# A split comparison and small maxima on VectorE beside a stream of indirect DMAs

## The chip, the cores and the metric

The kernel runs on one core of a Trainium2 chip. The metric is device time in microseconds (us), from one launch. A NeuronCore has TensorE (PE: matmuls, with its weight loads shown as PEld), VectorE (DVE), ScalarE (ACT), GpSimd (POOL) and SyncE (SP), which run their own instruction streams and meet at semaphores. Transfers are issued from SP, ACT and POOL; the indirect ones (gather and scatter by a list of indices) are issued from POOL.

## The reference

A graph has 6250 nodes with 48 features and 206,250 edges, sorted by destination. Two layers follow each other, each with a residual and a layer norm:

```
deg   = segment_sum(1, src) ;  dinv = rsqrt(deg)
x1    = layernorm(x + segment_sum(x[src] * dinv[src] * dinv[dst], dst))
gate  = silu(edge_attr @ W1.T + b1) @ W2.T + b2
gate += sum(emb[type[src]] * (emb[type[dst]] @ adaptW.T))
cw    = where(distance < 6, 0.5 * (cos(pi * distance / 6) + 1), 0)
msg   = gate * x1[dst] * (cw * node_vec[dst])
agg   = segment_sum(msg, src) / clip(segment_sum(node_vec[dst], src), 1e-8)
out   = layernorm(x1 + (layernorm(x1 + agg) * gamma + beta))
```

A segment sum is done as a matmul with a one-hot matrix: a comparison of indices with the numbers 0 to 127 yields ones where an edge belongs to a node, and TensorE multiplies by it.

## The kernel before, in words

Edges are cut into 101 tiles of 16 columns of 128 edges (NT = 101, G = 16). Three blocks follow each other.

The first (to about 290 us) counts degrees and prepares the tables in DRAM. The third (from about 2815 us) reads the scattered rows and adds them up per node. The change lies in the second, the loop over the tiles, from about 290 to 2815 us. There `over_tiles` (line 83) writes for each engine one list of steps; a step with lag k works in turn t on tile t - k. Six turns are unrolled in a hardware loop (U = 6). The order of the list is the order of the instructions on that engine.

In a turn each engine does this:

- POOL, `gather` (line 714): 16 indirect DMAs (line 722), one per column, each fetching 128 rows of the table by `gidx`; then `scatter` (line 726), one indirect DMA (line 730) that writes the routed rows of the tile 6 before. `gather` waits for `summed` and `gate_used` of the tile 6 before and for its indices.
- PE: the edge network (lines 747 and 759), `pick` (line 777), `routes` (line 821), `ranks`, and last `total` (line 856), which waits for the gathers of this turn and for the one-hot `oh_d`.
- ACT: copies out of PSUM and the splitting into bf16 parts (lines 882 to 970).
- DVE, in this order: `spots` (L1062, a minimum), `keys` (L1165), `product(0)` (L1195 to L1208), `normalize` in every second turn (L1109 to L1139), `steps_of_groups` (L1069), `onehots` (L1047, 2048 numbers a lane into `oh_d`), `buckets` (L1052, 816 numbers into `oh_b`), `route_onehots(0)` (L1089, eight comparisons of 896), `put_rows` (L1078), `add_early` (L1187) and `early_onehots` (L1176, 2048 and 640 numbers into `eoh`), `less_first` (L1148), `less_high(0)` (L1216), `product(1)`, `less_second` (L1156), `places` (L1057, 2048 numbers into `oh_t`), `less_high(1)` (L1216), `less_middle(0)` (L1224), `route_onehots(1)` (eight more of L1089), `less_middle(1)` (L1224).

`add_early` and `early_onehots` work only in the last 51 or so turns (EARLY_FROM = 46): they sum rows of a node group that are already complete.

Of the kernel before, what the change touches and what calls it, by code (L numbers as in the profile page):

```python
# [5 lines left out]
F32 = mybir.dt.float32  # L6
# [3 lines left out]
ALU = mybir.AluOpType  # L10
ACT = mybir.ActivationFunctionType
AX = mybir.AxisListType

P = 128
# [9 lines left out]
G = 16  # L24
# [8 lines left out]
U = 6  # L33
# [13 lines left out]
ECOLS = EARLY * R // P  # L47
# [18 lines left out]
def bc_mid(ap, n):  # L66

    return ap.unsqueeze(1).broadcast_to([ap.shape[0], n, ap.shape[1]])
# [7 lines left out]
def wait_apart(e, sem, value, passed):  # L76


    e.wait_ge(sem, value)
    e.sem_inc(passed, 1)  # L80
# [36 lines left out]
def since(i, s, n):  # L117

    return not isinstance(i, int) or U * i + s >= n
# [6 lines left out]
def build(nc, x, src, dst, edge_attr, edge_weight, node_type, node_vec, W1T, b1, W2T, b2,  # L126
# [14 lines left out]
    with ctx:  # L141
        def sb(name, shape, dt=F32, to=ctx):
            return to.enter_context(nc.sbuf_tensor(name, shape, dt))

        def ps(name, shape, dt=F32, to=ctx):
            return to.enter_context(nc.psum_tensor(name, shape, dt))

        def sem(name, to=ctx):
            return to.enter_context(nc.semaphore(name))

        passed = sem("passed")
        iota_f = sb("iota_f", [P, P])
# [8 lines left out]
        number = sb("number", [P, P, G], BF16)  # L161
        key16 = sb("key16", [P, K], BF16)
        bkt16 = sb("bkt16", [P, K], BF16)
        w16 = sb("w16", [P, K], BF16)
# [28 lines left out]
        with ExitStack() as ph:  # L193
# [67 lines left out]
            with nc.Block() as block:  # L261
                @block.sync
                def _(e):
                    e.dma_start(src_i[:, :], src).then_inc(src_in, 16)
                    e.dma_start(dst_i[:, :], dst).then_inc(dst_in, 16)
                    e.dma_start(nv[:, :], node_vec).then_inc(wl, 16)
                    e.dma_start(xin[:, :, :], x).then_inc(x_in, 16)
                    e.dma_start(b1c[0:C, :], b1).then_inc(wl, 16)
                    e.dma_start(b1c[C:2 * C, :], b1).then_inc(wl, 16)
                    e.dma_start(gam[:, :], gamma.broadcast_to([P, C])).then_inc(wl, 16)  # L270
                    e.dma_start(bet[:, :], beta.broadcast_to([P, C])).then_inc(wl, 16)
                    e.wait_ge(wz, 2)
                    for k in range(2):
                        e.dma_start(w1[RA * k:RA * (k + 1), C * k:C * (k + 1)], W1T).then_inc(wl, 16)
                        e.dma_start(w2[C * k:C * (k + 1), C * k:C * (k + 1)], W2T).then_inc(wl, 16)
                        e.dma_start(w2[2 * C:2 * C + 1, C * k:C * (k + 1)], b2).then_inc(wl, 16)
                    e.wait_ge(mapped, 1)
                    e.dma_start(src_pid, pid_i[:, :]).then_inc(stored, 16)
                    e.wait_ge(dst_done, 1)
                    e.dma_start(dst_pid, dst_i[:, :]).then_inc(stored, 16)  # L280
                    e.wait_ge(blank, 1)
                    e.dma_start(table0[NODE_ROWS:NODE_ROWS + P, :], zeros[:, 0:2 * EX].bitcast(F32)).then_inc(filled, 16)
                    for first in cleared:
                        e.dma_start(slots[R * first:R * (first + CAP - CLEAR), :].rearrange("(p a) c -> p (a c)", p=P),
                                    zeros[:, :]).then_inc(filled, 16)
                    e.wait_ge(types_got, 16 * NP2)
                    e.dma_start(queries.rearrange("p (h c) -> p h c", c=EM), tab[:, :, 0:EM]).then_inc(stored, 16)
                    for k, (a, b) in enumerate(PARTS):
                        e.wait_ge(lows, k + 1)
                        e.dma_start(table0[P * a:P * b, :].rearrange("(h l) c -> l h c", l=P),  # L290
                                    tab[:, a:b, EM:EM + EX]).then_inc(stored, 16)
                    e.wait_ge(wl, 16 * 11)
                    e.wait_ge(filled, 16 * (len(cleared) + 1))
                    e.wait_ge(stored, 16 * (len(PARTS) + 3))
# [268 lines left out]
        with ExitStack() as ph:  # L563
# [5 lines left out]
            oh_d = sb("oh_d", [P, 2, P, G], BF16, ph)  # L569
# [21 lines left out]
            eoh = sb("eoh", [P, P, ECOLS], BF16, ph)  # L591
            ethree = sb("ethree", [P, 3 * MW], F32, ph)
            epart = sb("epart", [P, MW], F32, ph)
            phid = ps("phid", [2 * C, 512], F32, ph)
            gate = ps("gate", [P, 512], F32, ph)
            pwin = ps("pwin", [P, 2, 512], F32, ph)
# [22 lines left out]
            erows_in, ecopied, emade, esummed, eout = (  # L619
                sem(n, ph) for n in ("erows_in", "ecopied", "emade", "esummed", "eout"))  # L620
# [18 lines left out]
            def visit(i, s):  # L639

                return U * i + s - EARLY_FROM
# [6 lines left out]
            def visits(i, s):  # L648

                return 0 <= visit(i, s) < NB if isinstance(i, int) else True  # L650

            def pair_of(i, s):

                return i * (U // 2) + s // 2

            with nc.Block() as block:
# [383 lines left out]

                @block.vector
                def _(e):
                    def onehots(i, s):
                        t = U * i + s
                        if since(i, s, 2):
                            e.wait_ge(summed, t - 1)
                        e.tensor_tensor(oh_d[:, s % 2], number[:, :, :], bc_mid(w16[:, bass.ds(t * G, G)], P),  # L1047
                                        ALU.is_equal).then_inc(ohd, 1)

                    def buckets(i, s):  # L1050
                        t = U * i + s
                        e.tensor_tensor(oh_b[:, :, :], number[:, 0:NB, :], bc_mid(bkt16[:, bass.ds(t * G, G)], NB),  # L1052
                                        ALU.is_equal).then_inc(ohb, 1)

                    def places(i, s):
                        e.wait_ge(row_in[s % 2], 16 * (pair_of(i, s) + 1))
                        e.tensor_scalar(oh_t[:, s % 2], oh_t[:, s % 2], iota_p[:, 0:1], None, ALU.is_equal  # L1057
                                        ).then_inc(oht, 1)

                    def spots(i, s):  # L1060
                        e.wait_ge(ranked, U * i + s + 1)
                        e.tensor_reduce(spot[:, s % 2, :], ranks_of.rearrange("p b q -> p q b"),  # L1062
                                        AX.X, ALU.min).then_inc(placed, 1)
# [103 lines left out]
                    def early_onehots(i, s):  # L1167
                        if not visits(i, s):
                            return
                        v = visit(i, s)  # L1170
                        wait_apart(e, ecopied, 2 * v + 1, passed)
                        if not isinstance(v, int) or v > 0:
                            e.wait_ge(esummed, v)
                        for a in range(0, ECOLS, G):
                            b = min(a + G, ECOLS)
                            oh = e.tensor_tensor(eoh[:, :, a:b], number[:, :, 0:b - a], bc_mid(emine[:, a:b], P),  # L1176
                                                 ALU.is_equal)
                        oh.then_inc(emade, 1)

                    def add_early(i, s):  # L1180
                        if not visits(i, s):
# [38 lines left out]
                    def less_middle(m):  # L1220
                        def step(i, s):
                            n = 2 * (U * i + s) + m
                            e.wait_ge(mid, n + 1)
                            e.tensor_tensor(parts[:, s % 2, m * HC:(m + 1) * HC, 2 * MW:2 * MW + C], val[:, m],  # L1224
                                            parts[:, s % 2, m * HC:(m + 1) * HC, MW:MW + C],
                                            ALU.subtract).then_inc(split_ok, 1)
                        return step

                    steps = [0]
# [31 lines left out]
                    with when(e, 1):  # L1261
                        over_tiles(e, NT, U, (spots, 5), (keys, 5), (product(0), 5), (normalize, 2), (steps_of_groups, 5),
                                   (onehots, 0), (buckets, 4), (route_onehots(0), 5), (put_rows, 5),
                                   (add_early, 7, EARLY_FROM), (early_onehots, 6, EARLY_FROM), (less_first, 2),
                                   (less_high(0), 5), (product(1), 5), (less_second, 2), (places, 4),
                                   (less_high(1), 5), (less_middle(0), 5), (route_onehots(1), 5),
                                   (less_middle(1), 5))
# [479 lines left out]
```

## Time and profile before

| | us |
|---|---|
| median of 3 runs | 3051.34 (3043.43 to 3051.47) |
| the profiled execution | 3027.21 |
| its span, first to last instruction | 3025.4 |
| POOL busy in the span | 2121.9 (70%) |
| DVE busy | 2404.3 (79%) |
| PE busy | 2250.1 (74%) |
| ACT busy | 1395.5 (46%) |

The span is what the profiler saw between the first and the last instruction. Engine, line and tile names are those of the program; the line is where the instruction was written. In a row of the timeline the first number is the start in us from the span's start, the second how long it took; what stands in brackets is the idle time of the engine before it and what ended it, and "issue" there means that it waited for nothing that the profile shows. Neighbouring instructions on DVE can overlap by up to 0.1 us, as the next starts while the last drains.

### The profile page before, as it was taken

What the parts mean: (1) busy time and instruction counts of PE and PEld (TensorE: products, weight loads), DVE (VectorE), ACT (ScalarE), POOL (GpSimd) and SP (SyncE); (2) the same over time, 40 slices, a digit from 0 to 9 for tenths busy, and PEclk for the clock granted to TensorE, in tenths of its full rate; (3) what the DMA queues carried; (4) which work ended last, traced back from release to release, by engine and by line L of the source; (5) the groups of instructions that cost most, each with busy time, mean ns of one, the idle gap of its engine ahead of it and who ended that gap; (6) DMA issues with size and microseconds to landing.
All of it is one profiled execution on the core that took longest, in us unless ns stands there. A gap on an engine that the chain in (4) does not pass through costs nothing. (4 is left out here: it accounts for less than half of the span.)

```text
span 3025.4 us, 73628 instructions
## 1 busy us (share of the span) xinstructions
PE 2250.1 (74%) x25909; PEld 1913.9 (63%) x25909; DVE 2404.3 (79%) x5424; ACT 1395.5 (46%) x2929; POOL 2121.9 (70%) x1852
## 2 busy tenths in 40 slices
PE   6980476678777787777787877787878787788475
PEld 5760365566666666655666666676767666667475
DVE  9994577777787777877788897888888878887698
ACT  7982244444444444444444444444444444445123
POOL 7506777877777777777777777777777777760165
PEclk9765688888888888988888898888989888979797
DMA  8405233333433434333344454444444444442896
GB/s 322 148 2 163 62 112 108 101 126 116 127 113 115 127 115 124 117 112 112 118 148 153 143 155 146 147 145 145 145 147 147 144 144 145 156 138 103 333 389 224
DMA packets 174987, 441.53 MB, mean 146 GB/s; under 512 B 92662, under 2 KB 92662, under 8 KB 154806
## 3 DMA queue, kind: packets, MB, share of 16 engines
q1 hardware_dynamic: 103754, 236.05, 23.4%
q0 software_dynamic: 67888, 194.98, 20.7%
q10 hardware_dynamic: 3004, 5.90, 0.6%
q8 instruction: 219, 3.59, 0.5%
q14 instruction: 122, 1.00, 0.1%
HBM read 292.51 MB, written 144.27 MB: 144 GB/s over the span
## 5 line engine op out<-in xcount | busy, mean ns | idle before, releaser
L722 POOL DMA_INDIRECT slot<-table,gidx x1616 | 1811.9, 1121 | 633.6 <-issue 620.2
L821 PEld LDWEIGHTS route<-parts,oh_r 128*128 128x128 bf16 x11312 | 764.9, 100 | 91.6 <-issue 66.9
L821 PE MATMUL route<-parts,oh_r 128*128 128x148 bf16 x11312 | 812.9, 232 | 3.2 <-DVE parts L1224 3.0
L1089 DVE TENSOR_SCALAR oh_r<-iota_r,spot 128x896 bf16<-128x896 f16 x1616 | 613.5, 451 | 74.4 <-PE route L821 74.4
L894 ACT ACTIVATE routed<-route 128x444 bf16<-128x444 f32 (+1 forms) x1010 | 507.9, 513 | 258.5 <-PE route L821 240.0
L856 PE MATMUL pwin<-slot,oh_d 128*128 128x144 bf16 x1616 | 167.6, 276 | 404.2 <-DMA slot<-table,gidx 372.1
L856 PEld LDWEIGHTS pwin<-slot,oh_d 128*128 128x128 bf16 x1616 | 147.8, 155 | 428.2 <-issue 270.0
L777 PEld LDWEIGHTS pwin<-win,oh_t 128*128 128x128 bf16 x4848 | 262.3, 117 | 200.6 <-issue 101.8
L777 PE MATMUL pwin<-win,oh_t 128*128 128x80 bf16 (+1 forms) x4848 | 277.0, 227 | 77.1 <-ACT ssum L904 71.6
L747 PE MATMUL phid<-attr,w 80*96 80x512 f32 x404 | 282.2, 789 | 44.4 <-issue 44.1
L1195 DVE TENSOR_TENSOR prod<-slot,got 128x256 f32<-128x256 f32 x202 | 84.6, 419 | 231.3 <-ACT parts L955 231.2
L759 PE MATMUL gate<-w,hid 97*128 97x96 f32 x1616 | 251.0, 305 | 1.6 <-ACT hid L882 1.6
L949 ACT ACTIVATE got<-pwin 128x640 f32<-128x640 f32 x202 | 142.0, 703 | 230.3 <-PE pwin L777 227.0
L759 PEld LDWEIGHTS gate<-w,hid 97*128 97x128 f32 x1616 | 225.9, 216 | 3.4 <-ACT hid L882 2.8
L730 POOL DMA_INDIRECT slots<-routed,sidx x101 | 116.5, 1153 | 115.1 <-ACT routed L894 76.9
L962 ACT ACTIVATE parts<-val 128x384 bf16<-128x384 f32 x202 | 104.5, 517 | 198.2 <-DVE val L1208 198.2
L882 ACT ACTIVATE hid<-phid,b1c 96x512 f32<-96x512 f32 x202 | 137.5, 681 | 119.9 <-PE phid L747 117.1
L1692 PE MATMUL acc<-rows,onehot 128*128 128x147 bf16 x1785 | 136.4, 239 | 68.1 <-issue 37.8
L323 ACT ACTIVATE by_col<-oh_hi 128x832 bf16<-128x832 bf16 x101 | 178.7, 1794 | 16.3 <-DVE oh_lo L463 12.5
L1176 DVE TENSOR_TENSOR eoh<-number,emine 128x2048 bf16<-128x2048 bf16 x102 | 102.8, 1057 | 99.8 <-ACT emine L981 99.6
L1692 PEld LDWEIGHTS acc<-rows,onehot 128*128 128x128 bf16 x1785 | 130.9, 143 | 73.6 <-issue 73.6
L356 PEld LDWEIGHTS deg<-by_col,oh_lo 128*128 128x128 bf16 x1616 | 108.9, 165 | 53.8 <-ACT by_col L323 53.2
(228 smaller groups left out, 3257.3 us busy)
## 6 DMA issues: line engine op xcount, KB each, us to landing
rows<-slots SPq DMA_DIRECT2D x51, 1295.0 KB, 8.8
oh_t<-dst_row SPq DMA_DIRECT2D x101, 512.0 KB
erows<-slots SPq DMA_DIRECT2D x51, 777.0 KB
attr<-in_edge_attr SPq DMA_DIRECT2D x101, 320.0 KB
slots<-zeros SPq DMA_DIRECT2D x53, 518.0 KB
slot<-table,gidx POOLq DMA_INDIRECT x1616
table<-tab SPq DMA_DIRECT2D x3, 676.0 KB, 5.9
weight_t<-weights SPq DMA_DIRECT2D x101, 8.0 KB
```

Of the source, the lines that this page charges most:

```text
L323: e.activation(by_col[:, s % OR], oh_hi[:, s % OR].rearrange("p b g -> p g b"), ACT.Copy).then_inc(laid, 1)
L722: e.indirect_dma_start(out=slot[:, s, g, :], out_offset=None, in_=table0, in_offset=bass.IndirectOffsetOnAxis(ap=gidx[:, s, g:g + 1], axis ...
L747: e.matmul(phid[:, :], w1[:, :], attr[:, s % 2, 512 * m:512 * (m + 1)], start=True, stop=True).then_inc(hidden, 1)
L759: mm = e.matmul(gate[:, 2 * C * k:2 * C * (k + 1)], hid[:, P * c:P * (c + 1)], w2[:, :], start=True, stop=True)
L777: mm = e.matmul(pwin[:, g // 4, first:first + n], oh_t[:, s % 2, m * HC + g, :], win[:, s, AT[k]:AT[k] + n], start=(k == 0), stop=(k == 2) ...
L821: mm = e.matmul(route[:, (NPH * m + phase) % 2, RC * (j - a):RC * (j - a + 1)], oh_r[:, c, slot_of, :], parts[:, s % 2, c, :], start=(c == ...
L856: mm = e.matmul(sums, oh_d[:, s % 2, :, g], rows[:, g, :], start=(g == 0), stop=(g == G - 1))
L882: e.activation(hid[0:2 * C, 512 * m:512 * (m + 1)], phid[:, :], ACT.Silu, bias=b1c[:, 0:1]).then_inc(hid_sb, 1)
L894: e.activation(routed[:, s % 2, RC * (HS * m + a):RC * (HS * m + b)], route[:, (NPH * m + phase) % 2, 0:RC * (b - a)], ACT.Copy).then_inc( ...
L949: e.activation(got[:, m].rearrange("p (b k) c -> p b k c", b=2), by_bank[:, :, :, 0:WX], ACT.Copy)
L1089: oh = e.tensor_scalar(oh_r[:, c], iota_r[:, :, :], spot[:, s % 2, c:c + 1], None, ALU.is_equal)
L1692: mm = e.matmul(acc[:, b % 2, 0:3 * MW], onehot[:, b % OS, :, c], rows[:, b % RS, c, 0:3 * MW], start=(c == 0), stop=(c == COLS - 1))
```

## The change

VectorE's comparison for `oh_d` is done in two halves, each of 64 of the 128 numbers (1024 elements a lane instead of 2048); the semaphore `ohd` is raised by the second. A helper `let_in` issues a maximum of two numbers per lane (a `tensor_reduce` of 128x2 to 128x1 in f32, without a wait and without a semaphore) into a small tensor of its own, `aside`. It stands behind each half of `oh_d`, behind `oh_b`, `oh_t`, both comparisons of `eoh`, and behind `less_middle(0)`. Nothing reads `aside`. That makes five such instructions in each of the 101 turns and two more in each of 51.

```
+            aside = sb("aside", [P, U, 8], F32, ph)
...
+                    def let_in(s, n):
+                        e.tensor_reduce(aside[:, s, n:n + 1], iota_f[:, 0:2], AX.X, ALU.max)
...
                     def onehots(i, s):
...
-                        e.tensor_tensor(oh_d[:, s % 2], number[:, :, :], bc_mid(w16[:, bass.ds(t * G, G)], P),
-                                        ALU.is_equal).then_inc(ohd, 1)
+                        for a in range(0, P, P // 2):
+                            oh = e.tensor_tensor(oh_d[:, s % 2, a:a + P // 2], number[:, a:a + P // 2, :],
+                                                 bc_mid(w16[:, bass.ds(t * G, G)], P // 2), ALU.is_equal)
+                            if a:
+                                oh.then_inc(ohd, 1)
+                            let_in(s, a // (P // 2))
                     def buckets(i, s):
...
+                        let_in(s, 2)
                     def places(i, s):
...
+                        let_in(s, 3)
...
(early_onehots)
-                        oh.then_inc(emade, 1)
+                            if b == ECOLS:
+                                oh.then_inc(emade, 1)
+                            let_in(s, 4 + a // G)
...
(less_middle)
+                            if m == 0:
+                                let_in(s, 7)
```

## Rows read from the trace of the kernel before

**Rows 1.** The page's head, and groups of POOL by line, 320 to 2600 us.
```profile
span 3025.4 us, 73628 instructions
...
L722 POOL DMA_INDIRECT slot<-table,gidx x1497 | 1673.3, 1118 | 476.5 <-issue 463.1 <-DMA gidx<-src_pid 9.7 <-DVE val L1201 3.7
L730 POOL DMA_INDIRECT slots<-routed,sidx x90 | 103.1, 1146 | 27.4 <-issue 26.8 <-DMA gidx<-src_pid 0.6
```

**Rows 2.** Two stretches of the loop: length, then each engine's busy us (instructions), clock, DMA.
```profile
320.00:1400.00 1080.00, 806.50 (x9136) 673.62 (x9137) 818.58 (x2075) 482.88 (x1077) 847.90 (x762) 0.86 0.38 114
1400.00:2600.00 1200.00, 955.91 (x11025) 811.27 (x11023) 992.89 (x2415) 551.48 (x1280) 928.41 (x825) 0.88 0.47 144
```

**Rows 3.** Timeline of POOL: two free gathers, two stretched, the last one.
```profile
1499.15 0.94 POOL L722 DMA_INDIRECT slot<-table,gidx  x1 [0.30 <-issue]
1500.40 0.94 POOL L722 DMA_INDIRECT slot<-table,gidx  x1 [0.30 <-issue]
...
1507.92 1.59 POOL L722 DMA_INDIRECT slot<-table,gidx  x1 [0.30 <-issue]
1509.81 1.11 POOL L722 DMA_INDIRECT slot<-table,gidx  x1 [0.30 <-issue]
...
2702.43 0.94 POOL L722 DMA_INDIRECT slot<-table,gidx  x1 [0.30 <-issue]
```

**Rows 4.** Timeline of DVE beside the gather of 1507.92.
```profile
1507.47 1.21 DVE L1047 TENSOR_TENSOR oh_d<-number,w 128x2048 bf16<-128x2048 bf16 x1
1508.61 0.57 DVE L1052 TENSOR_TENSOR oh_b<-number,bkt 128x816 bf16<-128x816 bf16 x1
```

**Rows 5.** Timeline of POOL: gathers held back longest, and the last beside oh_d.
```profile
346.14 5.17 POOL L722 DMA_INDIRECT slot<-table,gidx  x1 [0.30 <-issue]
...
950.94 2.27 POOL L722 DMA_INDIRECT slot<-table,gidx  x1 [0.30 <-issue]
...
1456.23 5.69 POOL L722 DMA_INDIRECT slot<-table,gidx  x1 [0.30 <-issue]
...
1711.52 2.52 POOL L722 DMA_INDIRECT slot<-table,gidx  x1 [0.30 <-issue]
...
2597.40 1.07 POOL L722 DMA_INDIRECT slot<-table,gidx  x1 [0.30 <-issue]
```

**Rows 6.** Timeline of DVE beside the gathers of 950.94, 1456.23 and 1711.52.
```profile
951.81 0.57 DVE L1052 TENSOR_TENSOR oh_b<-number,bkt 128x816 bf16<-128x816 bf16 x1
...
1457.07 2.98 DVE L1089 TENSOR_SCALAR oh_r<-iota_r,spot 128x896 bf16<-128x896 f16 x8
1459.98 0.20 DVE L1078 TENSOR_SCALAR sidx<-rank,iota_p 128x1 int32<-128x1 f32 x1
...
1461.13 0.42 DVE L1198 TENSOR_REDUCE logit<-prod 128x8 f32<-128x256 f32 x1
...
1711.36 2.00 DVE L1176 TENSOR_TENSOR eoh<-number,emine 128x2048 bf16<-128x2048 bf16 x2
```

**Rows 7.** Groups of DVE with their shapes: the comparison to be split, its neighbour, less_middle.
```profile
L1047 DVE TENSOR_TENSOR oh_d<-number,w 128x2048 bf16<-128x2048 bf16 x101 | 122.1, 1210 | 15.2 <-PE pwin L856 15.0
...
L1224 DVE TENSOR_TENSOR parts<-val,parts 128x384 bf16<-128x384 f32 x202 | 111.0, 550 | 0.0
...
L1052 DVE TENSOR_TENSOR oh_b<-number,bkt 128x816 bf16<-128x816 bf16 x101 | 57.4, 568 | 0.0
```

**Rows 8.** Timeline of DVE: a very small instruction and the one behind it.
```profile
1522.56 1.00 DVE L1062 TENSOR_REDUCE spot<-rank 128x16 f32<-128x816 f32 x1
1523.47 0.19 DVE L1165 COPY parts<-key 128x16 bf16 x1
1523.55 0.42 DVE L1195 TENSOR_TENSOR prod<-slot,got 128x256 f32<-128x256 f32 x1
```

**Rows 9.** Waits of PE from 700 to 1500 us: us in total, times, longest.
```profile
PE pwin L856 <- DMA slot<-table,gidx: 138.6, 31, 8.8
```

**Rows 10.** Waits of PE, then of DVE, from 1500 to 2400 us.
```profile
PE pwin L856 <- DMA slot<-table,gidx: 84.0, 34, 5.3
...
DVE eoh L1176 <- ACT emine L981: 61.9, 22, 5.9
```

## The prediction

> **What bounds the kernel now.** I first asked which engine never waits inside the loop. The groups of POOL from 320 to 2600 us show it [rows 1]: 1497 gathers and 90 scatters are busy for 1673.3 + 103.1 = 1776 us, and of the idle 476.5 + 27.4 = 504 us nearly all is "issue". The timeline tells what that idle time is: 0.30 us ahead of each gather [rows 3], and 1587 x 0.30 = 476 us. So POOL takes one indirect DMA after another and waits for hardly anything else: it sets the pace, although VectorE and TensorE are as busy in the same stretches [rows 2]. The waits of TensorE say the same from the other side: `total` waits for the gathered rows 31 times in 800 us and 34 times in 900 us, nearly once a turn, for 138.6 and 84.0 us [rows 9, 10].
>
> A free gather takes 0.94 us and the next starts 1.25 us later [rows 3]. A turn of 17 such would be 21.2 us. It is longer, since many gathers are stretched: 1673.3 - 1497 x 0.94 = 266 us in the 2280 us [rows 1], to which the scatters add some 14. That 280 us is all that the change can win on POOL; with 94 turns in the stretch it is 3.0 us a turn.
>
> What stretches them is read by laying the two timelines side by side. The gather of 1507.92 ends at 1509.51, 0.83 us behind the end of `oh_d` (1508.68) [rows 3, 4]. The gather of 1456.23 ends at 1461.92, 0.79 us behind the start of the first `TENSOR_REDUCE` that follows [rows 5, 6]. So a gather does about 0.15 to 0.2 us, then needs something that a long VectorE comparison holds, and needs some 0.75 us after it got it. In both of these cases VectorE ran on at its usual pace meanwhile (`oh_b` 0.57 against its mean of 0.568 [rows 4, 7]): the way is needed for an instant, and VectorE loses nothing by giving it.
>
> The end of an instruction does not always open the way. The gather of 1507.92 got in between `oh_d` and `oh_b`; that of 950.94 did not, and ended 0.83 us behind the end of `oh_b` (952.38) [rows 5, 6]; that of 1456.23 was passed over at the end of `oh_d`, `oh_b`, all eight `oh_r` and the four instructions behind them. Such starved gathers of over 5 us number 8, the first at 346.14 and the last at 1456.23 [rows 5].
>
> Going through the timeline from 320 to 2600 us with this point (0.19 us behind a gather's start), I put the 280 us down to the VectorE instruction that ran there. `oh_d`: 93 gathers, the first at 346.14 and the last at 2597.40 [rows 5], 90 us, of which the 8 starved make 37. The `oh_r` trains: 350 gathers, 71 us, such as the 0.17 us of 1509.81 [rows 3]. `eoh`: 44 gathers, 33 us, such as the 1.58 us of 1711.52 [rows 5, 6]. `less_middle`: 86 gathers, 26 us. `oh_t`: 75 gathers, 18 us. The rest, f32 products and subtractions, 42 us.
>
> **The change part by part.** If a gather's need falls anywhere in a held stretch of L us with equal chance, it waits L/2 on average and the chance is L/1.25, so a turn pays L x L / 2.5.
>
> *`oh_d` in halves, with maxima.* The slope between 816 and 2048 elements is (1210 - 568) / 1232 = 0.52 ns an element [rows 7], so a half of 1024 is 0.68 us, and 0.60 us from start to start, since neighbours overlap (`oh_d` 1.21 long, next start after 1.14 [rows 4]). Now: one stretch of 1.2 us and one of 0.57. If the boundary always opened this would be (1.44 + 0.3) / 2.5 = 0.7 us a turn; never opened, the first need falls on average 0.62 us into the 1.77, and the gather waits 1.14 us. Measured is 90 / 94 = 0.96. Then: three stretches of 0.6, 0.6 and 0.5: (0.36 + 0.36 + 0.25) / 2.5 = 0.39 us a turn. Gain 0.57 us x 94 = 54 us. Bounds: if no maximum ever opens more than a plain boundary does, the starved 37 us stay and the rest falls from 53 to 37 us, a gain of 16; at most all 90 go.
>
> *The maximum in `eoh`.* The comparisons of 1.2 and 0.7 us become separate stretches: (1.44 + 0.49) / 2.5 = 0.77 us against 33 / 47 turns = 0.70 now. By the formula nothing is won; only the cases like 1711.52, which missed the middle opening, about a dozen of the 44, gain 0.6 us each. I take 6 us; bounds 0 and 15.
>
> *Behind `less_middle(0)`.* It ends a run of f32 work before the second `oh_r` train. One 0.47 us stretch costs 0.09 a turn, 8 us for 94 turns, and there are two; 26 us are paid now. I take 7 us; bounds 0 and 20.
>
> *Behind `oh_t`.* The opening there works already as far as I see (75 gathers, 0.25 us each; the formula for 0.75 us gives 0.22 a turn, 21 us). I take 0; bounds -3 and 8.
>
> *What stays.* The 71 us in the `oh_r` trains and the 42 us of the f32 work are untouched.
>
> *What VectorE pays.* A maximum of two numbers: the nearest rows are a reduce of 816 at 1.00 us and a copy of 16 at 0.19, behind which the next starts after 0.08 us [rows 8]. I take 0.08 us; bounds 0.08 and 0.19. Five a turn, and the split adds 0.06: 0.46 us a turn, 0.62 with the two of `eoh`. Over 101 and 51 turns that is 46 + 8 = 54 us of VectorE's time (up to 120). What hides it is the wait for POOL. In 700 to 1500 us `total` waits 138.6 us in some 33 turns, 4.2 us a turn; in 1500 to 2400, 84.0 in 37, 2.3 a turn [rows 9, 10]. POOL's turn shrinks by 0.7, VectorE's loop grows by 0.6: 1.3 of the 2.3 are used. So the second half is near the edge but not over it. Queued behind each maximum is only the next VectorE step; TensorE's `total` gets `ohd` about 0.15 us later, which lies inside its wait for the gathers. The cover ends with the last gather at 2703.37 [rows 3]: the drain of six turns pays 6 x 0.5 = 3 us.
>
> Sum: 54 + 6 + 7 = 67 us, less 3 for the drain, gives 64. From this I take off 12: in turns with the early sums VectorE already waits 61.9 us for ScalarE's `emine` in 900 us [rows 10], a loop that POOL does not set, and in some of these turns the end will not be POOL's. So -52 us, and the profiled execution of 3027.21 becomes 2975. The profiled execution lay 24 us below the median of the runs; I carry the difference over to the median: 3051.34 - 52 = 2999 us.
>
> **A rule against it.** The rows show a gather passed over at more than ten boundaries [rows 5, 6]. The Trainium skill, "SBUF — State Buffer", section "SBUF: two separate sides", says that the port pair shared by VectorE and GpSimd is an exclusive lock held for a whole instruction, and that the blocked side goes on at VectorE's end plus about 115 ns. By that rule a maximum between two comparisons opens nothing that the end of the comparison did not open. The 5.17 to 5.69 us of the starved gathers disagree; the 0.83 us behind `oh_d` and `oh_b` agree with its other half. Its result is the second rival below.
>
> **The rivals.**
>
> *More than forecast.* Gathers and VectorE's steps run in step with each other (the 0.30 us gap and the fixed order), so one removed stretch can free others: a gather that isn't late at `oh_d` may miss the `oh_r` train's first members too. If a third more goes, 67 becomes 95, less 3: 3051 - 92 = 2959. For: the starved gathers come in the same place each time. Against: the `oh_r` trains cost 0.2 us a gather whatever comes before.
>
> *The maxima open nothing.* A window of 0.08 us may be too short: `sidx` at 1459.98, another tiny instruction, did not help the starved gather [rows 6]. Then only the halves count: 16 us, less 3 for the drain: 3038. For: that row. Against: the first `TENSOR_REDUCE` let every one of the 8 in.
>
> *VectorE becomes the bound (slower).* Place: the turns from 46 on, in the chain `oh_r`, TensorE's routes, ScalarE's `emine`, `eoh`. From the point where a turn without POOL's wait takes as long as POOL's (24.5 us now, by 1200 us for 49 turns), the added 0.62 us count in full, and at 0.19 us a maximum, 7 x 0.19 + 0.06 = 1.4 us. Price: 55 x 0.62 = 34 us there and 3 in the drain, less the 16 us of the halves in the first turns: +21, 3072. For: `eoh` already waits for ScalarE. Against: `total` still waits for the gathers in 34 of 37 turns there.
>
> *Nothing changes.* A gather that no longer waits at `oh_d` waits in the train behind it: the halves' 16 us go to 0 and little else is left: 3048.
>
> **How the numbers follow.** Within 0.3% (3042 to 3060) is what this measurement can't tell from no change. Forecast 2999: 0.52. More: 0.13. The maxima open nothing (3038, its range reaches over 3042): 0.16. Nothing: 0.08. VectorE bound: 0.11. Faster: 0.52 + 0.13 + 0.11 of the 0.16 = 0.76; same: 0.05 + 0.08 = 0.13; slower 0.11. The forecast's own range, with the bounds of its terms, is 2965 to 3030. To hold 8 in 10 I take 2952 to 3048, which leaves out the slower rival and the far end of the better one.
>
> **What would show it.** Right: no gather above about 3 us in the loop; the mean of L722 falls from 1118 to about 1075 ns; POOL's idle time stays 0.30 us a gather; the last gather ends near 2650 instead of 2703; `total` still waits for the gathers; the maxima take under 0.2 us. The second rival: gathers of over 5 us remain. The third: idle time of POOL ahead of L722 that ends with `gate_used` or `summed`, and `total` no longer waits for the DMA. Wrong altogether would be L722's mean down and the span unchanged.

## The result, and the profile after

The change made the kernel slower: 3101.22 us median (3068.73 to 3109.05, 5 runs) against 3043.43 (3036.94 to 3051.47, 5 runs), a ratio of 1.0171 (95% interval 1.0111 to 1.0231). The forecast was 2999, with 3048 as its upper end. The profiled execution took 3068.73 us with a span of 3066.9, 41.5 more than [rows 1]. It was the fastest of the five; the other four took 3099.21 to 3109.05 us, and what they spent beyond it is in no trace. The medians lie 58 us apart, so some 16 of them stay unexplained.

The gathers of the changed kernel, over the whole span (`L723` is their line there; before, the gathers were 1811.9 us busy, mean 1121 ns, in the page's costliest group):

```profile
L723 POOL DMA_INDIRECT slot<-table,gidx x1616 | 1851.8, 1146 | 636.1 <-issue 623.9 <-DMA gidx<-src_pid 8.2 <-DVE val L1214 4.0
```

So GpSimd still sets the pace, its idle time ahead of the gathers is nearly what it was (636.1 us against 633.6), and the loss of this execution is in the gathers: 1851.8 - 1811.9 = 39.9 us more busy, for 41.5 us more span. The last gather moved by about the same amount, 44.1 us, from 2702.43 [rows 3] to:

```profile
2746.49 1.10 POOL L723 DMA_INDIRECT slot<-table,gidx  x1 [0.30 <-issue]
```

TensorE's `total` waits for them as before, in the same two stretches as [rows 9, 10], 700 to 1500 us and 1500 to 2400:

```profile
PE pwin L857 <- DMA slot<-table,gidx: 152.6, 31, 11.8
...
PE pwin L857 <- DMA slot<-table,gidx: 96.5, 30, 7.0
```

The gathers should have been shorter and are longer. The timelines say where. First a gather of POOL, then VectorE beside it:

```profile
1152.94 5.61 POOL L723 DMA_INDIRECT slot<-table,gidx  x1 [0.30 <-issue]
```

```profile
1152.61 0.67 DVE L1053 TENSOR_TENSOR oh_d<-number,w 128x1024 bf16<-128x1024 bf16 x1
1153.20 0.14 DVE L1046 TENSOR_REDUCE aside<-iota_f 128x1 f32<-128x2 f32 x1
1153.27 0.56 DVE L1061 TENSOR_TENSOR oh_b<-number,bkt 128x816 bf16<-128x816 bf16 x1
1153.76 0.14 DVE L1046 TENSOR_REDUCE aside<-iota_f 128x1 f32<-128x2 f32 x1
1153.82 2.98 DVE L1100 TENSOR_SCALAR oh_r<-iota_r,spot 128x896 bf16<-128x896 f16 x8
1156.72 0.20 DVE L1089 TENSOR_SCALAR sidx<-rank,iota_p 128x1 int32<-128x1 f32 x1
...
1157.32 0.41 DVE L1208 TENSOR_TENSOR prod<-slot,got 128x256 f32<-128x256 f32 x1
1157.76 0.42 DVE L1211 TENSOR_REDUCE logit<-prod 128x8 f32<-128x256 f32 x1
```

The gather came for its way at about 1153.13, in the second half of `oh_d`. It was passed over at two maxima (1153.20 and 1153.76) and through the train, and got on only at 1157.8, beside `L1211`. What sets `L1211` apart is that VectorE waits there for its own result: `prod` ended at 1157.73 and it starts at 1157.76. The maxima start while the instruction ahead of them still drains (1153.20 against an end of 1153.28) and the next comparison starts while they drain (1153.27 against 1153.34). VectorE never stands still around them.

There is a second kind of long gather, of which the kernel before has none from 320 to 2600 us. It starts 0.47 us behind the start of `oh_b`, so its need falls into the train, the eight `oh_r` comparisons, and it is held for 2.2 us, through about six of them:

```profile
649.10 3.18 POOL L723 DMA_INDIRECT slot<-table,gidx  x1 [0.30 <-issue]
```

```profile
648.63 0.56 DVE L1061 TENSOR_TENSOR oh_b<-number,bkt 128x816 bf16<-128x816 bf16 x1
...
649.18 2.97 DVE L1100 TENSOR_SCALAR oh_r<-iota_r,spot 128x896 bf16<-128x896 f16 x8
```

Of gathers over 3 us from 320 to 2600 us, the changed kernel has 12 of over 5 us, the first at 346.13 and the last at 1484.07, and 8 of 3.17 or 3.18, the first at 649.10 and the last at 1689.07, where [rows 5] stood for 8 in all. These few are nearly the whole loss: what the 20 take beyond 0.94 us each is 75.8 us, against 36.8 for the 8 of before, so 39.0 of the 39.9 us.

VectorE's price was as estimated: 607 maxima of 146 ns, the next start 0.07 us after a maximum's own.

```profile
L1046 DVE TENSOR_REDUCE aside<-iota_f 128x1 f32<-128x2 f32 x607 | 88.6, 146 | 0.0
```

### The profile page after: what moved, and what is told of

Same layout as the page of the kernel before. It is cut to its first block and busy times, and to the rows that moved or that the text cites. A ratio compares the mean times of both kernels' runs of the same rounds, so it can differ in the third digit from the quotient of the medians.

```text
span 3066.9 us, 74234 instructions
## 1 busy us (share of the span) xinstructions
PE 2234.4 (73%) x25807; PEld 1914.7 (62%) x25909; DVE 2442.6 (80%) x6132; ACT 1399.2 (46%) x2929; POOL 2159.9 (70%) x1852
## 5 line engine op out<-in xcount | busy, mean ns | idle before, releaser
L723 POOL DMA_INDIRECT slot<-table,gidx x1616 | 1851.8, 1146 | 636.1 <-issue 623.9
L1100 DVE TENSOR_SCALAR oh_r<-iota_r,spot 128x896 bf16<-128x896 f16 x1616 | 605.9, 445 | 63.2 <-PE route L822 63.2
L905 ACT ACTIVATE ssum<-pwin 128x144 f32<-128x144 f32 x101 | 28.1, 278 | 275.7 <-PE pwin L857 267.2
```

The costliest lines, as they stand in the source:

```text
L723: e.indirect_dma_start(out=slot[:, s, g, :], out_offset=None, in_=table0, in_offset=bass.IndirectOffsetOnAxis(ap=gidx[:, s, g:g + 1], axis ...
L1100: oh = e.tensor_scalar(oh_r[:, c], iota_r[:, :, :], spot[:, s % 2, c:c + 1], None, ALU.is_equal)
```

## The experiments

Two questions: do the maxima let gathers in, and what makes the kernel slower, the boundaries or VectorE's added time? For the first, the gathers whose need fell clearly into `oh_d` (into its first half, where it is halved) were counted in each trace, over the loop, and how many of them got on at its end. One counts that started before the end of `oh_d` by 0.28 us or more and still ran 0.6 us behind it; it got on there if it ended within 0.95 us of it, as all that do end 0.81 to 0.83 us behind it.

### Where TensorE sets the pace

The first two groups of runs fell on chips where every kernel took over 4000 us (the kernel before: 4055.82 and 4166.3 us medians). A profile of the kernel before, taken there, shows why; the busy times of its two stretches (compare [rows 2]):

```profile
320.00:1400.00 1080.00, 612.91 (x6104) 501.76 (x6136) 555.43 (x1408) 312.55 (x727) 574.51 (x534) 0.74 0.28 78
1400.00:2600.00 1200.00, 761.22 (x7375) 630.01 (x7407) 658.61 (x1635) 362.28 (x861) 616.27 (x562) 0.74 0.31 89
```

And VectorE's and TensorE's longest waits there, over the whole span (us in total, times, longest):

```profile
DVE oh_r L1089 <- PE route L821: 574.9, 79, 19.1
...
PE route L821 <- issue: 499.2, 387, 9.8
```

TensorE was late with the routing matmuls, waiting for nothing that the profile shows, at a granted clock of 0.74 against 0.86 and 0.88. There VectorE's time counts and GpSimd's does not, so these ratios say nothing on the result, and the theories below that assume GpSimd's pace are not tested by them; the counts of openings hold all the same.

**e1_halves, f1_halves** (the halves, no maxima).

```
for a in range(0, P, P // 2):
    oh = e.tensor_tensor(oh_d[:, s % 2, a:a + P // 2], ...)
    if a:
        oh.then_inc(ohd, 1)
```

> The comparison for oh_d in two halves, no maxima. Theory A (GpSimd is passed over at the boundary of two VectorE instructions that follow without a stop, and a new boundary is a new chance to be passed over): the halves alone already cost, ratio to before 1.005 to 1.015, with more than 8 gathers over 5 us and the mean gather above 1121 ns. Theory B (the maxima's own time on VectorE is the loss): 0.995 to 1.002, mean gather 1105 to 1120 ns, 8 or fewer over 5 us.

> The halves alone, on a chip where GpSimd may set the pace. Theory A (each boundary of VectorE instructions without a stop is a chance for GpSimd to be passed over): ratio 1.003 to 1.015 and more gathers over 3 us than the 8 of before. Theory B (only VectorE's added time costs): 0.997 to 1.003.

Measured 1.006 (1.0025 to 1.0095) and 1.0055 (1.0015 to 1.0095). Of 61 waiting gathers 17 got on at the end of the first half. No gather of the loop is over 3 us, against theory A; in 97 of e1_halves' 101 turns VectorE pauses behind `oh_b`, in the trace of [rows 1] in 46.

**e2_maxima, f2_maxima** (`oh_d` whole, every maximum kept).

> All maxima, the comparison for oh_d whole. Theory A: the maxima too are boundaries without a stop, so 1.003 to 1.012, with gathers over 3 us that before did not have. Theory B: 1.010 to 1.017, nearly all of the changed kernel's loss. If instead only the halving is harmful: 0.99 to 1.00 and 8 or fewer gathers over 5 us.

> The maxima alone. Theory A: 1.003 to 1.012 where GpSimd sets the pace, with gathers over 3 us. Theory B: 1.01 to 1.02 on any chip (506 maxima).

Measured 1.0218 (1.0167 to 1.0269), above every range named, and 1.0129 (1.0065 to 1.0193). Of 106 waiting gathers 52 got on at the end of `oh_d`, with a maximum behind it. In the control **f0_before** it was 23 of 66 without one.

> The kernel before once more, as a control with a profile of its own on the same chip. Every theory: ratio 0.995 to 1.005. If GpSimd sets the pace on this chip, the mean gather is near 1121 ns, total waits for the gathers nearly once a turn and about 8 gathers last over 5 us; if TensorE does, the mean gather is below 1080 ns and VectorE waits for TensorE's routes for hundreds of us.

It measured 1.0006 (0.9951 to 1.0061).

**e3_stops, f3_stops** (the kernel before; VectorE waits for its own instruction).

```
 e.tensor_tensor(oh_d[:, s % 2], ...).then_inc(ohd, 1)
+e.wait_ge(ohd, t + 1)
 ...
 e.tensor_tensor(oh_b[:, :, :], ...).then_inc(ohb, 1)
+e.wait_ge(ohb, t + 1)
```

> The kernel before, with VectorE waiting for its own oh_d and for its own oh_b before it goes on (two waits a turn, no maxima, no halves). Theory A: a real stop of 0.1 to 0.2 us lets GpSimd in every time: no gather over 3 us, mean gather down from 1121 to about 1090 ns, ratio 0.978 to 0.992. Theory C (what counts is how long VectorE holds its port, not a stop): as before within 0.3%. Theory B: 101 times 2 times 0.15 us are added, 1.005 to 1.01.

> VectorE waits for its own oh_d and its own oh_b. Theory A: where GpSimd sets the pace no gather lasts over 3 us, the mean gather is below 1100 ns and the ratio is 0.98 to 0.992. Theory B: 1.005 to 1.015, as where TensorE sets the pace.

Measured 1.0141 (1.0078 to 1.0203) and 1.0164 (1.0088 to 1.0241): slower than even theory B said, presumably because each added wait is on the path there. But all 101 of 101 waiting gathers got on at the end of `oh_d`.

**e4_long** (the changed kernel, each maximum over 128 numbers).

```
-e.tensor_reduce(aside[:, s, n:n + 1], iota_f[:, 0:2], AX.X, ALU.max)
+e.tensor_reduce(aside[:, s, n:n + 1], iota_f[:, :], AX.X, ALU.max)
```

> The changed kernel with a maximum of 128 numbers in place of two, about 0.2 us from start to start in place of 0.07. Theory C' (a maximum opens the way when it is long enough): gathers over 3 us are gone, the mean gather falls below 1110 ns and the ratio is 0.98 to 0.995. Theory A: still gathers over 3 us, ratio 1.01 to 1.025. Theory B: 607 times 0.13 us more, 1.03 to 1.04.

Measured 1.0409 (1.0361 to 1.0457). All 28 of 28 got on at the end of the first half. So a maximum of two opens nothing for certain, a real stop does, and so does a long maximum there.

### Where GpSimd sets the pace

The other two groups fell on chips like that of the forecast (before: 3033.86 and 3040.37 us medians). The same four kernels, then four more:

| kernel | ratio (95% interval) | mean gather, ns | gathers busy, us | idle ahead of them, us | over 3 us | span, us |
|---|---|---|---|---|---|---|
| before | 1 | 1121 | 1811.9 | 633.6 | 8 | 3025.4 |
| changed | 1.0171 (1.0111 to 1.0231) | 1146 | 1851.8 | 636.1 | 20 | 3066.9 |
| g3_halves | 1.0039 (1.002 to 1.0058) | 1139 | 1839.8 | 617.4 | 10 | 3037.7 |
| g4_maxima | 1.0137 (1.0114 to 1.016) | 1160 | 1874.8 | 618.5 | 14 | 3074.0 |
| g2_long | 1.0091 (1.0067 to 1.0116) | 1122 | 1812.4 | 663.4 | 14 | 3056.2 |
| g1_stops | 0.9879 (0.9858 to 0.99) | 1090 | 1762.0 | 661.4 | 0 | 2999.0 |
| h1_time | 1.0062 (1.0041 to 1.0083) | 1132 | 1829.6 | 630.3 | 13 | 3046.7 |
| h3_ohb | 0.9929 (0.9901 to 0.9957) | 1114 | 1799.8 | 633.8 | 0 | 3020.2 |
| h4_ohd | 0.9886 (0.9856 to 0.9917) | 1107 | 1789.6 | 638.4 | 0 | 3010.8 |
| h2_all | 0.9898 (0.9869 to 0.9927) | 1068 | 1726.4 | 700.5 | 0 | 3005.3 |

The ratio is that of the medians of several runs; the other columns are of the one profiled execution, over its whole span, but for the gathers over 3 us, which are counted from 320 to 2600 us.

**g3_halves.** 

> The halves alone. If GpSimd sets the pace: gathers over 3 us are more than the 8 of before, ratio 1.003 to 1.015. Where TensorE sets the pace: 1.003 to 1.009 again.

Met, at the low end. Of 31 gathers waiting in the first half 11 got on at its end. The gathers take 27.9 us more, but 16.2 us of idle time ahead of them went, so the span grew by 12.3.

**g4_maxima.** 

> The maxima alone. They open nothing. If GpSimd sets the pace they are hidden for the most part: 1.000 to 1.012, with gathers over 3 us behind oh_b, as 649.10 in the changed kernel. Where TensorE sets the pace: 1.012 to 1.022 again.

Just above what was expected. The halves' 0.4% and the maxima's 1.4% add up to about the change's 1.7%; the gathers' busy time does not add up so (27.9 and 62.9 us more alone, 39.9 together). Of 65 gathers waiting in `oh_d` 29 got on at its end, with a maximum there; before it was 26 of 52, without one.

These shares hide that for most gathers it is no matter of chance. The table sorts them by how long before the end of the whole `oh_d` they started. It has every gather whose need, taken as 0.19 us behind its start, falls into `oh_d`:

| start before the end, us | got on, no maximum | a maximum | a stop |
|---|---|---|---|
| 0.19 to 0.22 | 0 of 88 | 0 of 33 | 95 of 95 |
| 0.22 to 0.35 | 67 of 67 | 28 of 29 | 108 of 108 |
| 0.35 to 0.45 | 0 of 17 | 0 of 5 | 15 of 15 |
| 0.45 to 0.65 | 25 of 25 | 4 of 4 | 16 of 16 |
| 0.65 to 0.735 | 0 of 7 | 1 of 14 | 8 of 8 |
| 0.735 to 0.775 | 29 of 30 | 19 of 22 | 57 of 57 |
| 0.775 to 0.92 | 8 of 24 | 4 of 9 | 19 of 19 |
| 0.92 to 0.99 | 9 of 99 | 10 of 52 | 121 of 121 |
| 0.99 to 1.21 | 15 of 15 | 13 of 13 | 24 of 24 |

(No maximum: before, f0_before, h1_time, h3_ohb. A maximum: g4_maxima, f2_maxima. A stop behind `oh_d`: g1_stops, h2_all, h4_ohd, e3_stops, f3_stops.) Where VectorE goes straight on, a few hundredths of a microsecond in the gather's start decide, and they decide nearly alike with and without a maximum. So these counts show no effect of the maximum at this boundary. Why the outcome alternates so is not shown.

**g2_long.** 

> The changed kernel with maxima of 128 numbers. They open the way too (every gather held by a half got in at its end), but cost 0.2 us each. If GpSimd sets the pace: no gather over 3 us, mean gather near 1080 ns, but VectorE's turn grows by 1.1 us: ratio 0.985 to 1.005. Where TensorE sets the pace: 1.035 to 1.045 again.

Met only in the opening behind the first half of `oh_d`, where all 42 of 42 got on. The ratio lies above the range, the mean gather is 1122 ns and not near 1080, and 14 gathers are over 3 us: 9 that waited in `oh_b` lasted 3.57 us, held into the train, although a long maximum stood behind `oh_b`, and 5 more lasted 4.4 to 4.5 us. A long maximum is not a sure opening. This is also the one kernel that is slower without longer gathers: they are busy 0.5 us more than before, and the idle time ahead of them grew by 29.8 us, with 164.8 us of maxima on VectorE.

**g1_stops.** 

> VectorE waits for its own oh_d and oh_b. So far a gather held back by oh_d got in at its end every time behind such a stop, and less than half the time at a plain boundary. If GpSimd sets the pace on this chip: no gather over 3 us, mean gather below 1100 ns against 1121, ratio 0.98 to 0.993. If the time of VectorE counts after all there: 1.003 to 1.01. Where TensorE sets the pace: 1.01 to 1.02 again.

Met: 0.9879, and the fastest profiled execution of all (3001.19 us). The gathers of its loop from 320 to 2600 us, beside [rows 1]:

```profile
L722 POOL DMA_INDIRECT slot<-table,gidx x1512 | 1646.8, 1089 | 507.1 <-issue 487.2 <-DMA gidx<-src_pid 16.6 <-DVE val L1203 3.4
```

15 gathers more in the same time. One of them that is held, and VectorE beside it:

```profile
1438.62 1.77 POOL L722 DMA_INDIRECT slot<-table,gidx  x1 [0.30 <-issue]
```

```profile
1438.35 1.21 DVE L1047 TENSOR_TENSOR oh_d<-number,w 128x2048 bf16<-128x2048 bf16 x1
1439.60 0.58 DVE L1053 TENSOR_TENSOR oh_b<-number,bkt 128x816 bf16<-128x816 bf16 x1
```

It ends at 1440.39, 0.83 us behind the end of `oh_d` (1439.56). The stop itself shows here only as 0.04 us between that end and the start of `oh_b`, where without it the two overlap by 0.07 [rows 4]; in most turns it is 0.12 or 0.15 us. Here 54 of 54 got on at the end of `oh_d`.

The gathers take 49.9 us less than before, but the idle time ahead of them is 27.8 us more, and the span is 26.4 us shorter. GpSimd already waits for others here, so only a part of what the gathers gain arrives.

A pause need not be put in to work. Over the loops of all ten kernels of the table, a gather of over 1.0 us met an end of a VectorE instruction, 0.22 us or more behind its own start, with at least 0.03 us of pause behind it 1515 times and got on at 1513 of them. At ends where the next instruction overlapped the last, it got on 4478 times and was passed over 2294 times.

The last four runs ask why the maxima alone make gathers wait longer, and what each stop is worth.

**h1_time** (before, with five maxima in a row behind the copy `L1165`, away from every long comparison).

```
 e.tensor_copy(parts[:, s % 2, :, RC - 1], key16[...]).then_inc(split_ok, 1)
+for n in range(5):
+    let_in(s, n)
```

> Five maxima a turn in a row behind the copy L1165, whose neighbours are a reduce out of PSUM and prod, so that no long comparison gets another boundary. Theory T (VectorE comes later to its own waits, the natural stops shrink, and gathers are passed over more): mean gather 1135 to 1160 ns, ratio 1.006 to 1.014, as the maxima alone. Theory A (only a boundary next to a held stretch does harm): mean gather 1115 to 1130 ns, ratio 0.998 to 1.005.

1.0062, with 13 gathers over 3 us, such as one of 5.35 us at 1348.45.

The measured values fall between the two theories (a mean gather of 1132 ns, just under T's range and just over A's; a ratio whose interval reaches into both), so the run does not choose between them. It shows that 505 maxima away from every long comparison cost 0.6%, and how: the gathers are busy 17.7 us more, and VectorE did not become the bound, as GpSimd's idle time did not grow. What the 13 long gathers take beyond 0.94 us each is 58.2 us against 36.8 for the 8 of before, which is more than all of it. Theory T's reason is not borne out: the train follows `oh_b` without a pause in 54 turns, just as in 54 before. But of the gathers waiting at the end of `oh_b` in those turns none of 14 got on, against 4 of 12 before. By the table under g4_maxima that is a matter of when they start, and the maxima shift VectorE's instructions against the gathers; that this shift is the whole cause is argued, not shown. What the rest of the maxima's 1.4% comes from was not tested apart.

**h3_ohb, h4_ohd** (one stop each).

> The stop behind oh_b alone. It stands ahead of the train of eight oh_r and so catches every gather that would starve: no gather over 3 us, but the misses at the end of oh_d stay (0.5 us each, some 20). Mean gather 1095 to 1105 ns, ratio 0.989 to 0.995.

> The stop behind oh_d alone. Every gather held by oh_d gets in at its end, but one whose need falls into oh_b can be passed over and starve through the train: a few gathers over 3 us. Mean gather 1095 to 1110 ns, ratio 0.99 to 0.997.

Both met in part: each stop alone removes all long gathers from 320 to 2600 us. h3_ohb's ratio is in its range, its mean gather of 1114 ns is above it. h4_ohd's mean is in its range, and its ratio of 0.9886 is better than expected. Behind `oh_d` the stop also catches the misses at that boundary (61 of 61 get on, against 25 of 61 with the stop behind `oh_b` alone), and brings what both bring. The starving that was expected for a gather whose need falls into `oh_b` came once in h4_ohd, late in the loop, in a turn without `oh_d`:

```profile
2681.07 4.04 POOL L722 DMA_INDIRECT slot<-table,gidx  x1 [0.30 <-issue]
```

```profile
2680.82 0.57 DVE L1053 TENSOR_TENSOR oh_b<-number,bkt 128x816 bf16<-128x816 bf16 x1
2681.32 2.98 DVE L1090 TENSOR_SCALAR oh_r<-iota_r,spot 128x896 bf16<-128x896 f16 x8
```

**h2_all** (stops behind `oh_d`, `oh_b`, `oh_t`, the whole `eoh` and `less_middle(0)`).

> A stop (VectorE waits for its own instruction) behind oh_d, oh_b, oh_t, the second part of eoh and less_middle(0). If every stop opens the way: mean gather 1075 to 1090 ns against 1090 with two stops, ratio 0.982 to 0.99. If the added 0.5 us a turn bring VectorE to its limit: 0.99 to 1.0.

The gathers get shorter still, 1068 ns, but the ratio is 0.9898, no better than with two. From 320 to 2600 us POOL does one gather more than in g1_stops, 1513, and its idle time has grown from 507.1 to 543.7 us:

```profile
L722 POOL DMA_INDIRECT slot<-table,gidx x1513 | 1612.3, 1066 | 543.7 <-issue 513.9 <-DMA gidx<-src_pid 27.6 <-DVE val L1206 2.1
```

What GpSimd gains in the gathers beyond g1_stops it loses ahead of them. g1_stops, h4_ohd and h2_all all beat the kernel before and the changed one, and can't be told from each other.

## Why the prediction was wrong

What bounds the kernel was right, for this change. In all ten kernels of the table the span ends 318 to 328 us behind the last gather, and the 25 ns a gather that the change added are 1616 x 0.025 = 40 us of the 41.5 in the profiled execution. It is not the only bound: g2_long lost 30.8 us of span to idle time of GpSimd, and of the 49.9 us that g1_stops took off the gathers only 26.4 arrived in the span (36.0 by the medians). The sum took off 12 us of 64 for the turns that GpSimd does not end, which was rather too little.

That a gather needs an opening for an instant and that plain boundaries often don't give it was right too, and so was the place of the starved gathers: with both stops all of them are gone, and 50 us of gather time with them.

The step that failed is "Then: three stretches of 0.6, 0.6 and 0.5 ... Gain 0.57 us x 94 = 54 us". It took for granted that each maximum opens the way. The starved gathers that got on beside a `TENSOR_REDUCE` were put down to the instruction, when what let them in was the pause ahead of it, in which VectorE waits for its own result. Nor did it let every one of the 8 in, as the prediction says: 6 got on at the end of `prod`, where the pause is 0.03 us, as at the shortest stops of g1_stops, and those of 346.14 and 393.47 at the end of the `oh_r` train, where there is none. The counts: 29 of 65 behind a maximum, 26 of 52 behind a plain end, 54 of 54 behind a stop. The row that told of this was in [rows 6]: `sidx`, as tiny and as closely followed, opened nothing for the gather of 1456.23. I gave that rival 0.16, and priced it by the stretches alone, at a gain of 13.

The bound under it failed as well. "If no maximum ever opens more than a plain boundary does ... a gain of 16" treated a new boundary as at worst useless. The halves alone cost 0.4%, with 28 us more in the gathers. A gather passed over at the first boundary was passed over at the next: of the gathers waiting in the changed kernel's first halves, 9 of 22 got on at its end and none at the second's. So halving a stretch does not halve the wait. The formula L x L / 2.5, which spreads the needs evenly, does not hold either: at a plain end some starts always got on and others never.

The third failure is "What hides it is the wait for POOL". VectorE's added time did not become the bound, but it is not without effect on the gathers: h1_time costs 0.6% though it touches no long comparison, by five more starved gathers. So it is not the slower rival that was named, and `total` waited for the gathers about as often as before (31 and 30 times in the two stretches, against 31 and 34). The slower side came by a mechanism that was not listed, the gathers themselves getting longer.

The rule that was weighed came out half right. The Trainium skill, "SBUF — State Buffer", section "SBUF: two separate sides", lets the blocked side go on once VectorE's instruction ends. The runs agree where VectorE stops there (54 of 54, the gather ending 0.83 us later) and disagree where the next instruction follows at once (26 of 52).

## What to carry to other kernels

Where GpSimd's indirect DMAs set the pace, their mean duration is the number to watch, and the longest of them show where VectorE shuts them out. A short instruction put in between opens nothing for certain; a pause of VectorE does, even one of 0.03 us, and a wait for its own result makes one. One such wait behind the longest comparison was worth 1.1% here where GpSimd set the pace, while a second helped little and five brought nothing more; where TensorE set it, two such waits cost 1.4 and 1.6%. Before spending a hidden engine's idle time, check that its instructions don't hold back the engine that sets the pace.

## What the runs showed that was not expected

The same kernel took 3034 to 3043 us on some chips and 4056 to 4166 us on others, where TensorE's stream of route matmuls came with gaps of mostly 1.0 to 1.2 us (some of 1.8) that nothing in the profile explains, and the sign of an edit differed between them: the two stops made it 1.2% faster on the one kind and 1.4 and 1.6% slower on the other. What causes the gaps stays open.
